# A Trainium2 kernel of a tokenizer, a state space model and a mixture of experts: coefficient steps placed in other units, constants loaded in two parts

## The reference, cut to what matters

```
x: (64 images, 64 channels, 64 x 64 pixels)
1 tokenizer: patches of 4 x 4 pixels; the mean of a patch makes the query, its 16 pixels
  make keys and values (each after a layer norm); softmax over the 16 pixels; projection
  h = patch mean + attention @ proj_w.T + proj_b
2 state space model along the tokens of an image, with dt = 1/tokens, s = 1/(1 + dt*dt*a):
  x_new = s*x - dt*s*a*z + dt*s*Bu        z_new = dt*s*x + s*z + dt*dt*s*Bu
  out = g*sigmoid(g) + h,  g = gelu(z @ W_C.T + h @ W_D.T + biases)
  h = layernorm(h + out)
3 mixture: shared MLP + 4 experts (two of them chosen per token); h = layernorm(h + mixture)
```

## Time and profile before

| | us |
|---|---|
| median of 3 runs (lowest, highest) | 1020.51 (1019.67, 1021.63) |
| the profiled execution's own time | 1021.32 |
| its span in the trace | 1019.5 |
| PE, DVE, ACT, POOL busy | 943.5, 761.7, 501.4, 436.1 |

### The profile page before, as it was taken

The page is one execution under the profiler, slowest core; times in us unless marked ns, Lnnn a source line. Parts: engine busy times, 40 slices in busy tenths (PEclk is TensorE's granted clock), DMA queues, the critical chain, the costliest instruction groups (busy, mean ns, idle before and its releaser), DMA issues.

```text
span 1019.5 us, 24614 instructions
## 1 busy us (share of the span) xinstructions
PE 943.5 (93%) x9608; PEld 368.8 (36%) x9608; DVE 761.7 (75%) x1290; ACT 501.4 (49%) x799; POOL 436.1 (43%) x259
## 2 busy tenths in 40 slices
PE   4569999999999999999999989996999999999996
PEld 1114344343434334343434443232333333333332
DVE  6678787878778787878878776998566766766664
ACT  3335454554545454454545412265465664655753
POOL 3237676777767677776767720000110100101000
PEclk9769999999999999999999999998899999999999
DMA  9128878787887878787887742000000000000000
GB/s 384 33 65 234 263 212 264 212 247 230 240 257 218 262 214 247 228 241 251 225 256 217 215 110 58 0 1 0 0 12 21 10 10 21 10 16 15 10 22 22
DMA packets 64007, 141.47 MB, mean 139 GB/s; under 512 B 22576, under 2 KB 22576, under 8 KB 55728
## 3 DMA queue, kind: packets, MB, share of 16 engines
q1 hardware_dynamic: 63920, 140.18, 47.1%
HBM read 68.85 MB, written 4.19 MB: 72 GB/s over the span
## 4 chain that ended last, share of the span: by engine, by line
PE 82%; DVE 11%; issue 3%; DMA 1%; POOL 1%; ACT 1%; SPq 0%; DVEq 0%; POOLq 0%
PE ring L798 20%; PE bank_ms L770 11%; PE qp L835 11%; PE bank_sq L770 5%; PE ring L991 5%; DVE sb_prodv L1152 4%; PE ring L1002 4%; PE bank_ms L1032 3%; PE qp L969 2%; PE bank_sq L991 2%; PE ring L985 2%; PE ring L932 2%; PE bank_ms L1002 2%; PE bank_ms L1024 2%; PE bank_sq L1011 1%
## 5 line engine op out<-in xcount | busy, mean ns | idle before, releaser
L798 PE MATMUL ring<-sb_arena,sb_wqkv 64*64 64x512 f32 x2048 | 269.4, 609 | 37.8 <-DVE sb_prodk L1121 20.2
L1152 DVE TENSOR_TENSOR sb_prodv<-ring,sb_wbc 128x1024 f32<-128x1024 f32 x128 | 154.1, 1207 | 32.6 <-PE ring L798 30.2
L1121 DVE TENSOR_TENSOR sb_prodk<-ring,sb_qbuf 128x1024 f32<-128x1024 f32 x128 | 153.4, 1220 | 20.6 <-PE ring L798 18.1
L405 POOL TENSOR_TENSOR sb_rows<-sb_arena 128x2048 f32<-128x2048 f32 x31 | 141.4, 4562 | 14.8 <-DMA sb_arena<-x 14.8
L534 POOL TENSOR_TENSOR sb_parts_q<-sb_arena,sb_const 128x512 fp32r<-128x512 f32 x15 | 15.6, 1040 | 305.6 <-ACT sb_arena L654 305.6
L835 PEld LDWEIGHTS qp<-sb_prodv,sb_tok_w 64*64 64x64 f32 x4096 | 119.6, 133 | 54.7 <-issue 51.4
L835 PE MATMUL qp<-sb_prodv,sb_tok_w 64*64 64x128 f32 x4096 | 128.4, 269 | 2.5 <-DVE sb_prodv L1152 2.5
L577 ACT ACTIVATE sb_xsq<-sb_arena 128x2048 f32<-128x2048 f32 x64 | 118.5, 1899 | 6.9 <-DMA sb_arena<-x 6.9
L798 PEld LDWEIGHTS ring<-sb_arena,sb_wqkv 64*64 64x64 f32 x2048 | 59.1, 133 | 172.9 <-issue 83.4
L501 POOL TENSOR_TENSOR sb_score<-sb_score,sb_smx 128x512 f32<-128x512 f32 x32 | 41.0, 1281 | 105.1 <-DVE sb_smx L1135 105.1
L407 POOL TENSOR_TENSOR sb_rows<-sb_rows 128x1024 f32<-128x1024 f32 x31 | 73.9, 2384 | 2.4
(11 more groups left out here) (198 smaller groups left out, 1489.1 us busy)
## 6 DMA issues: line engine op xcount, KB each, us to landing
sb_arena<-x SPq DMA_DIRECT2D x64, 1024.0 KB, 8.7
sb_wbc<-sb_wgt SPq DMA_DIRECT2D x256, 256.0 KB, 5.7
out<-sb_arena SPq DMA_DIRECT2D x64, 64.0 KB, 1.9
sb_rest_w<-rest_w SPq DMA_DIRECT2D x1, 918.5 KB, 22.1
sb_const<-const SPq DMA_DIRECT2D x1, 520.5 KB, 8.1
sb_tok_w<-tok_w SPq DMA_DIRECT2D x1, 260.5 KB, 2.8
```

The lines of the kernel that those rows point to most:

```text
L405: eng.tensor_tensor(rows[:, :, :, :], pix[:, :, 0:8], pix[:, :, 8:16], ALU.add).then_inc(sum8_ready, 1)
L798: mm = pe.matmul(ring[slot][C * half:C * half + C, i, :], image_block(w, i), x[C * i:C * i + C, m, half, c], start=True, stop=True)
L1121: dve.tensor_tensor(by_pixel(prodk[:, c]), by_pixel(ring[c % 2][:, :, :]), q[:, :, None, :].to_broadcast([P, 2, N_PIX, G32]), ALU.mult).th ...
L1152: dve.tensor_tensor(prodv[:, :, :, G32 * c:G32 * (c + 1)], by_pixel(ring[k % 2][:, :, :]), by_pixel(wbc[:, c]), ALU.mult).then_inc(values_ ...
```

## The change

Of the sixteen coefficient steps the first four stay where they are. The steps 4 to 15 leave the hand-written start and go to the ends of DVE's steps 0 (one), 1, 2, 3 (two each), 28, 29 (two each) and 30 (one), each behind `pixel_var(n+2)`. The constants go in two transfers: columns 0 to 528 ahead of unit 0's pixels, the rest last of the first loads, with a semaphore of its own for which POOL waits ahead of L525.

```diff
--- before.py
+++ after.py
@@ -68,6 +68,7 @@
 N_PIECE = HP // CH
 STORE = 4 * 16
 VALUE_ORDER = (0, 2, 1, 3)
+FREE_STEPS = {0: (4, 5), 1: (5, 7), 2: (7, 9), 3: (9, 11), 28: (11, 13), 29: (13, 15), 30: (15, 16)}
 N_RES = 4
 
 
@@ -196,6 +197,7 @@
 
         const_in = sem("const_in")
         tok_in = sem("tok_in")
+        select_in = sem("select_in")
         rest_in = sem("rest_in")
         coefs = sem("coefs")
         x_in = [sem(f"x_in{m}") for m in range(NF)]
@@ -460,11 +462,12 @@
                                          ).then_inc(weights_spread[c], 16)
 
             sp.dma_start(tok_w[:, :], t["tok_w"]).then_inc(tok_in, 16)
+            sp.dma_start(const[:, 0:K_SEL], t["const"][:, 0:K_SEL]).then_inc(const_in, 16)
             load(0)
-            sp.dma_start(const[:, :], t["const"]).then_inc(const_in, 16)
             for u in range(1, NF):
                 load(u)
             sp.dma_start(rest_w[:, :], t["rest_w"]).then_inc(rest_in, 16)
+            sp.dma_start(const[:, K_SEL:K_END], t["const"][:, K_SEL:K_END]).then_inc(select_in, 16)
             spread_weights(0)
             for n in range(UNITS):
                 if n + 1 < UNITS:
@@ -522,6 +525,7 @@
             pool.wait_ge(rest_in, 16)
             pool.wait_ge(projected_mm, UNITS)
             pool.tensor_copy(exact[:, H_B3:H_SEL], b3).then_inc(weights_rounded, 1)
+            pool.wait_ge(select_in, 16)
             pool.tensor_copy(exact[:, H_SEL:H_ONES], const[:, K_SEL:K_END]).then_inc(weights_rounded, 1)
             pool.tensor_copy(exact[:, H_ONES:H_END], const[:, K_ONES:K_CEN]).then_inc(weights_rounded, 1)
             pool.memset(route[:, :].bitcast(F32), 0.0).then_inc(route_cleared, 1)
@@ -1216,7 +1220,6 @@
 
             query_var(0)
             query_scaled(0)
-            free_steps(4, 13)
             pixel_var(0)
             for c in range(NC):
                 key_products(0, 0, c)
@@ -1226,8 +1229,6 @@
             score_sum(0)
             score_inverse(0)
             query_scaled(1)
-            free_steps(13, L)
-            assert n_coefs[0] == N_COEFS
             pixel_var(1)
             def step(n, m):
                 nxt = not isinstance(n, int) or n + 1 < UNITS
@@ -1259,12 +1260,15 @@
                 value_products(n, m, 3)
                 if nxt2:
                     pixel_var(n + 2)
+                if isinstance(n, int):
+                    free_steps(*FREE_STEPS.get(n, (0, 0)))
                 if not nxt:
                     for j in range(EARLY, BEFORE_TOKENS):
                         scan_ahead(0, j)
                         scan_on(0, j)
 
             pipeline(dve, step, UNITS)
+            assert n_coefs[0] == N_COEFS
             tokens(UNITS - 1, (UNITS - 1) % NF)
 
             def fix_z(h, j):
```

## The result

| | before | after |
|---|---|---|
| median of the runs | 1020.62 us | 1048.28 us (1044.70 to 1048.53, four runs) |
| the profiled execution, its span | 1021.32, 1019.5 us | 1044.70, 1042.8 us |
| PE, DVE busy in the span | 943.5, 761.7 us | 949.1, 778.4 us |

The account below looks back on a forecast made before the run. PE bounds the tokenizer's steady part, DVE's coefficient steps the start. Start -24.3, constants +0.2, steps at new places +36.6 and clock +12.5 give +25.0 on 1021.32: 1046.3, median 1045.5 us, range 1030 to 1052.

Parts of the forecast that it names:

- Gain of the start: Start of the kernel: moving the coefficient steps out saves 24.3 us, bounds 18.4 and 26.
- first group: Nine coefficient steps ahead of pixel_var(0): without them score_scale(0) comes at 29.6 in place of 40.22, 10.6 us gained.
- clock of unit 1: Unit 1, first key product to score_scale: 6.9 us in place of 9.94 with PE at half clock, 3.0 us gained.
- Constants: Start: 0.27 MB of constants ahead of unit 0's pixels delay them 0.7 us, of which 0.2 shows (0 to 0.5).
- Stalls: Ends of steps 0 to 3 and 28: POOL's patch sums hold cacc and cv, costing 5.3 and 4 x 7.5 us.
- Step 29: End of step 29: no POOL patch sums are left, so two free steps cost 1.3 us.
- Who holds whom: DVE's steps beside POOL: cacc and cv are held until POOL's running operation ends; cz is not.
- Rival 2: DVE slips between two POOL additions, cv and cz ahead of POOL: 27.6 in place of 36.6, 1036.5 us; chance 0.10.
- Clock: Behind each of five stalls PE's clock falls to half: 2.5 us each, 12.5 us in all (0 to 17.5).
- Rival 1: The stalls stand but PE's clock doesn't fall, the holes being shorter: +12.5, 1033.0 us; chance 0.12.
- Rivals 3 and 4: 3: POOL not in patch sums, steps run free, 1003.7 us, chance 0.12. 4: second group's 10.7 not gained, 1056.2, 0.06.
- second group: Three coefficient steps at the start from 46.31: without them pixel_var need not wait until 57.05, 10.7 us gained.

Follow-up runs that it names:

- run 9: Changed kernel with the first nine moved steps back ahead of pixel_var(0) and the other three at the end of step 30: 1007.67 us, ratio 0.9871 to the kernel before.
- run 6: Changed kernel with the constants in one transfer behind unit 0's pixels, as before the change: 1045.18 us.
- run 10: Changed kernel with two moved steps at the end of step 28 and the other ten at the end of step 30: 1010.14 us, ratio 0.9888.
- run 5: Changed kernel unaltered, executed again with a second profile: 1047.15 us.
- run 7: Kernel before with only the constants split into two transfers: 1021.90 us, ratio 1.0007 to the kernel before.
- Run 1: Changed kernel with POOL waiting, ahead of its patch sums, until DVE has done the coefficient steps: 1008.72 us, ratio 0.9878 to the kernel before.
- run 4: Changed kernel with the same steps in the same units, but ahead of score_scale(n+1) in place of DVE's step end: 999.14 us, ratio 0.9792.
- run 2: Changed kernel with 5 or 7 unneeded full matmuls on PE inside the five holes, DVE and POOL untouched: 1035.71 us.

## Why the prediction was right, point by point

- **Gain of the start.** Forecast 24.3: first group 10.6, second 10.7, clock of unit 1 3.0. The first profile gives 40.22 - 29.45 = 10.8, 10.7 and 3.0, together 24.5, and run 9 shows the last two apart. It isn't safe in each execution: in runs 6 and 10 the clock fell in unit 1, in which my sum had it full, and 2.2 us were gone (2.5 by `pixel_var(2)`).
- **Constants.** Forecast 0.2 with a bound of 0.5. This term was mis-sized. In the first profile ACT used the pixels 0.57 us later (9.50 against 8.93, forecast 0.7) and DVE 0.1 later (9.56 against 9.46), as I had it; in other profiles DVE's use was up to 2.6 us late. By runs 5 and 6 the part costs some 2 us in the median, by run 7 1.2, with no cost at all within run 7's interval. The step that failed is the rate: I took 0.7 us from bytes and a mean rate, and didn't ask how long the queue takes to issue the pixels behind the constants (3.9 to 5.5 us), with DVE only 0.5 us behind the landing.
- **Stalls.** Forecast PE later by 5.3 and 4 x 7.5, 35.3 in all; PE's third key quarter came 5.3, 7.5, 7.5, 7.75 and 7.5 us later behind `pixel_var` than in the earlier trace rows, 35.5 in all, with holes of 5.15, 7.29, 7.30, 7.56 and 7.29. Run 1 shows the cause by taking POOL away from the place, run 4 by taking the steps away from POOL. Step 29 cost 1.4 (forecast 1.3) and step 30 nothing on DVE.
- **Who holds whom.** The Trainium skill's rule that an add with two SBUF inputs contends as well (SBUF — State Buffer, section "Who interferes with whom") is borne out by `cz`, 0.58 us beside POOL's addition; I had read from the earlier trace rows that it was never held. The sum didn't hang on it. To start just ahead of POOL didn't save `cv`: at 55.90 against POOL's 55.91 it was held as it was at 54.45 against 54.47 before. Rival 2 fell: DVE passed between two of POOL's operations once in nine steps beside them, and then `cz` paid for it.
- **Clock.** Forecast 2.5 per stall. Measured 1.7 to 2.0 in the first profile, by what the distances have over the stall, 1.65 to 1.91 in run 2, 2.9 in run 10. The mechanism is shown by run 2; the size was one third too high for the changed kernel's five, and a sixth fall, 1.4 us behind step 30, wasn't in the sum. Together 9.5 and 1.4, 10.9 where 12.5 were forecast. Rival 1 fell.
- **Rivals 3 and 4.** POOL's phase against DVE stayed within 0.2 us of what it was in the units before (its L407 began 1.23 us ahead of `pixel_var(2)` there, 93.54 against 94.77, and 51.30 against 52.53 here). The second group's gain came whole.
- **Sum.** The first profile: -24.5 (the pixels' 0.1 is in it) + 36.9 (35.5 and step 29's 1.4) + 10.9 = +23.3, as measured on the spans. The median lies 3.6 above that profile; run 5's profile, which took as long, has 2.1 of late pixels, 1.0 of PE's slower first matmuls and 1.0 in the four units, and what the other executions have isn't shown. That 25.0 lies so near both 23.3 and 27.7 is in part luck: the clock's price was too high by 3.0 for five falls, the sixth fall gave 1.4 of it back, and late pixels and a slower start, of which my sum had 0.2, brought most executions above it.

## What to carry to other kernels

Work of a few elements isn't free on VectorE when GpSimd streams beside it: ask which of its operands lie in SBUF (the key products, with one input in SBUF and one in `ring`, kept their 1.22 us beside the same additions), and look for the phase of the unit in which GpSimd is between two jobs or VectorE is waiting for PE. Here the same twelve steps cost 48 us with the clock, or nothing in the length of the units, depending on the place within the unit alone. And when a transfer is put ahead of one that something waits for within half a microsecond, time several executions, since a single profile can show it early.

## What I had not expected

PE's clock also fell where the idle stretches were short: 1.14 and 2.47 us with 2.2 us of matmuls between them (after, 625 to 631 us, the fall within the second), and a single one of 1.71 us in unit 1 of run 6. The same stretches left it at 1.00 in the kernel before and in the changed kernel's first profile respectively. And the queue took 3.9 us in some executions and 4.6 to 5.5 in others to issue the same eight pixel transfers when the constants went ahead of them, and 2.96 to 3.14 us for its last six in all four profiles with the constants behind unit 0's pixels.
